# A decoder layer on one core: gathering and starting the first expert tile inside the last batch's attention heads

## The chip, the cores and the metric

The kernel runs on one core of one Trainium2 chip. The metric is the device time of one execution in microseconds, the median of several runs. It is written in Bass: every engine has its own instruction stream in program order, and streams meet only in semaphores. TensorE is PE in the rows, VectorE DVE, ScalarE ACT, GpSimd POOL, SyncE SP.

## What is computed

One post-norm decoder layer over 16 sequences of 100 tokens with 256 features, in fp32: windowed self-attention, cross-attention to 361 context rows with 16 heads, and a mixture of 8 experts of which each token takes 2.

```python
def reference(x, ctx_1024, ...):
    x = _layernorm(x + _L0_attn_ref(x, ...))
    x = _layernorm(x + _L0_xattn_ref(x, ctx_1024, ctx_1024, ...))
    x = _layernorm(x + _L0_ffn_ref(x, ...))
    return x

def _L0_ffn_ref(x, Ws, bs, Wg, Wu, Wd):
    logits = xt @ Ws + bs
    topk_w, topk_idx = jax.lax.top_k(logits, K)          # K = 2 of E = 8
    topk_w = jax.nn.softmax(topk_w, axis=-1)
    combine = jnp.sum(jax.nn.one_hot(topk_idx, E) * topk_w[..., None], axis=1)
    h = jax.nn.silu(xt @ Wg[e]) * (xt @ Wu[e])           # for every expert e, 256 -> 688
    out = sum over e of (h @ Wd[e]) * combine[:, e]
```

## The kernel before

The run has three stages.

**Self-attention** takes the 16 batches in eight pairs and leaves x1 and its transpose in DRAM.

**Cross-attention** is a software pipeline, written out by hand: iteration `i` runs 16 heads, and between the heads stand, at fixed places, the key scores and the exponentials of batch `i`, the query scores (for the maxima) and values of batch `i + 1`, the keys and queries of batch `i + 2`, and the tail of batch `i - 1`: last heads weighed (`weigh_values`), turned (`turn_weighed`), divided by the softmax sums on VectorE (`normalise`), turned again (`turn_attended`), projected (`project`), residual, mean and variance, the inverse root on GpSimd, `apply` (which makes x2), the store of x2 to DRAM, `turn_x2`, and the router product `logits`. The last iteration in which TensorE runs heads is `i = NB - 1 = 15`: there no batch is left for query scores, keys, queries or values. After it follows a stretch written out by hand for every engine, in which the tail of batch 15 is mixed with the first expert tiles.

**Routing** runs beside this in five groups of batches (`GROUPS`). Per group: logits with bias, comparison of all pairs, the two best experts (`chosen`, array `M`), ranks of the tokens within their experts (`rank_rows`, on TensorE), the place of each (`scaled`, `place`, `rounded`, `split`), one-hot rows (`hot`) and their product, the lists of tokens by tile (`enter`). Four tiles that are already full after eight batches, `Step(0, 0)` to `Step(0, 3)`, are known at the end of iteration 14 (`first_tiles` writes their rows `gat` and experts `expert_of`); they use rows of the first 800 tokens only. The other 28 tiles of `TILES = 32` are known after the last batch: `used`, `number_tiles`, `select`, `pack`.

**Expert tiles.** A tile is 128 tokens of one expert. For a tile `t`: `weights` loads 1.4 MB of gate and up weights into one of four buffers `W` (SyncE's queue); `gather` copies the tile's token numbers and issues an indirect DMA of its 128 rows of x2 from DRAM into one of four slots `xs` (GpSimd's queue); `turn_rows` transposes the rows on TensorE into PSUM bank `B_X` and `rows_out` copies them to SBUF on ScalarE; `gate_up` makes three parts of products, 4, 3 and 4 chunks of 128 columns (part 0 the gate, in bank `B_G`, part 1 the mixed one in `B_C`, part 2 the up part in `B_U`; a chunk is four passes in the trace, since fp32 takes two for each of two halves of the features); `silus` is the activation on ScalarE, `hidden` the product of both on VectorE; `down` is the product with the down weights in SBUF (`WD`), after a load of the expert's number into a register; `weigh` scales it by the token's weight and an indirect DMA adds it to DRAM. In the loop TensorE does, for `u = 0, 1, ...`: part 0 of tile `u + 2`, `down(u)`, `turn_rows(u + 3)`, and parts 1 and 2 of tile `u + 2`.

What sets the order around the change: TensorE is in order, so a `turn_rows` that waits for a gather holds everything behind it. In before, the turning of tile 0 stands right behind the router product of batch 14, after the heads. GpSimd is in order too: in iteration 15 it does `split_maximum(15, 1)`, the weights of routing group 2, the sum of x1 and bias (L1326), then the inverse root of batch 14 (L1338, L1340), constants of the tile stage (L654 to L658), and then the four early gathers (L664, L667). On SyncE the weights of tiles 0 and 1 are loaded at the start of iteration 15, x2 of batch 14 is stored, then the weights of tiles 2 and 3 follow.

## Time and profile before

| | before |
|---|---|
| median of 3 runs (lowest to highest) | 691.37 us (690.7 to 695.07) |
| the profiled execution | 694.28 us, its span 692.5 us |
| TensorE busy | 630.1 us (91%) |
| VectorE, ScalarE, GpSimd busy | 376.0, 312.4, 284.1 us |
| chain that ended last | TensorE 75%, VectorE 10%, DMA 3%, GpSimd 3% |
| mean granted TensorE clock | 0.962 |

How to read it: a busy share is an average over three stages. Self-attention goes to about 120 us of the span, cross-attention to about 408, the expert tiles to about 675, and a last normalisation follows. In a timeline a row is a group of equal instructions that follow each other, with the start, the time from first start to last end, and in brackets the idle time ahead of it and what ended it. The end of a matmul is modelled and lies somewhat behind the start of the next one, so a stretch of TensorE is best measured from start to start.

### The profile page before, as it was taken

The page shows a single profiled execution, that of the slowest core. Times are in us where ns is not written, and L with a number is a line of the kernel's source. Part 1 is how long each engine was busy: PE and PEld are TensorE (multiplying, and loading weights), DVE is VectorE, ACT ScalarE, POOL GpSimd, SP SyncE. Part 2 cuts the span into 40 slices and gives each one's busy share as a digit, 9 for nine tenths or more (in the row PEclk, how much of TensorE's full clock was granted, in tenths as well). Part 3 has the DMA queues.
Part 4 walks back from the last instruction along what each step waited for, and adds up shares of the span by engine and source line. Part 5 has one row for each costly group of instructions (what it writes and reads, how often), then busy time and mean ns, then how long its engine had stood idle before and what let it go on. Part 6 is the DMA issues. An engine that isn't in the chain of part 4 may idle for free.

```text
span 692.5 us, 16844 instructions
## 1 busy us (share of the span) xinstructions
PE 630.1 (91%) x5898; PEld 535.7 (77%) x5899; DVE 376.0 (54%) x989; ACT 312.4 (45%) x807; POOL 284.1 (41%) x511
## 2 busy tenths in 40 slices
PE   6989886999999998999899858999999999999970
PEld 5988874667777776777677648999999999999960
DVE  2878775777777876787777737222222222222214
ACT  2344424477777765777667645121221222122213
POOL 2535354333353449343954241443344334432220
PEclk9999988899999999999999979999999999999995
DMA  8332103556666644444343282877767777677105
GB/s 244 101 81 68 53 25 102 162 177 188 191 191 190 188 130 122 135 122 115 104 105 96 64 312 87 289 208 223 234 216 203 219 233 230 196 216 240 39 0 190
DMA packets 73666, 108.85 MB, mean 157 GB/s; under 512 B 9786, under 2 KB 51330, under 8 KB 72834
## 3 DMA queue, kind: packets, MB, share of 16 engines
q1 hardware_dynamic: 67458, 100.40, 46.9%
q0 software_dynamic: 6144, 7.61, 6.2%
q8 instruction: 38, 0.62, 0.4%
q14 instruction: 26, 0.21, 0.1%
HBM read 73.25 MB, written 12.44 MB: 124 GB/s over the span
## 4 chain that ended last, share of the span: by engine, by line
PE 75%; DVE 10%; issue 4%; ACT 3%; DMA 3%; POOL 3%; SPq 1%; DVEq 0%; POOLq 0%; ACTq 0%
PE ps L727 22%; PE ps L768 12%; PE ps L1459 6%; PE ps L1511 6%; PE ps L1533 5%; PE ps L1486 5%; PE ps L1470 4%; PE ps L1554 2%; PE ps L1519 2%; PE ps L1379 2%; POOL r_ln L353 1%; PE ps L1436 1%; PE ps L1390 1%; PE ps L707 1%; DVE a_mx L1988 1%
## 5 line engine op out<-in xcount | busy, mean ns | idle before, releaser
L1999 DVE TENSOR_REDUCE cmx<-ps 100x1 f32<-100x361 f32 x256 | 134.5, 531 | 68.5 <-PE ps L1459 64.2
L727 PE MATMUL ps<-xsT,W 128*128 128x128 f32 x1408 | 165.2, 276 | 0.0
L727 PEld LDWEIGHTS ps<-xsT,W 128*128 128x128 f32 x1408 | 161.3, 193 | 0.4 <-issue 0.3
L1771 ACT ACTIVATE cpr<-ps 128x300 f32<-128x300 f32 x256 | 104.8, 420 | 58.1 <-PE ps L1470 57.5
L910 DVE TENSOR_SCALAR y<-ps,wt 128x256 f32<-128x256 f32 x32 | 15.5, 484 | 143.3 <-PE ps L768 135.0
L685 POOL DMA_INDIRECT accd<-y,si x32 | 51.2, 1600 | 102.1 <-DVE y L910 101.3
L1459 PE MATMUL ps<-st 96*100 96x361 bf16 x256 | 86.0, 339 | 5.5 <-DVE cmx L1999 2.3
L768 PE MATMUL ps<-WD,hT 128*128 x384 | 88.3, 380 | 1.4 <-DVE y L910 1.4
L1470 PEld LDWEIGHTS ps<-st 120*128 120x128 bf16 x768 | 63.1, 102 | 32.1 <-issue 9.2
L1470 PE MATMUL ps<-st 120*128 120x100 bf16 x768 | 77.1, 209 | 3.6 <-ACT st L1776 1.7
L768 PEld LDWEIGHTS ps<-WD,hT 128*128 128x128 f32 x384 | 70.5, 190 | 10.0 <-issue 1.8
L1288 POOL COPY parts<-parts 128x722 bf16<-128x722 bf16 x32 | 28.5, 891 | 77.8 <-DVE parts L2006 77.8
L800 ACT ACTIVATE sg<-ps 128x512 f32<-128x512 f32 x32 | 19.1, 597 | 91.0 <-PE ps L727 91.0
L1533 PE MATMUL ps<-cwv_sb,cx 128*128 128x256 f32 x192 | 54.0, 405 | 0.0
L1459 PEld LDWEIGHTS ps<-st 96*100 96x100 bf16 x256 | 32.5, 127 | 24.8 <-DVE cmx L1999 13.3
L1511 PE MATMUL ps<-cx,cwk_sb 128*128 128x361 f32 x128 | 49.2, 509 | 0.0
L1486 PE MATMUL ps<-cpr,cva 128*32 128x100 f32 (+1 forms) x1536 | 47.6, 257 | 0.0
L667 POOL DMA_INDIRECT xs<-x2d,gi x32 | 32.8, 1025 | 25.6 <-POOL gi L664 25.6
L792 ACT ACTIVATE wt<-xs 128x8 f32<-128x8 f32 x32 | 6.7, 208 | 68.8 <-PE ps L707 68.8
L1486 PEld LDWEIGHTS ps<-cpr,cva 128*32 128x32 f32 (+1 forms) x1536 | 33.1, 111 | 5.5 <-issue 0.5
L1533 PEld LDWEIGHTS ps<-cwv_sb,cx 128*128 128x128 f32 x192 | 34.1, 197 | 2.9 <-issue 0.2
L1253 POOL TENSOR_TENSOR xb<-x_sb,bv_bc 100x512 f32<-100x512 f32 x8 | 10.2, 1275 | 48.8 <-DVE a_xr L1952 43.1
(238 smaller groups left out, 1020.0 us busy)
## 6 DMA issues: line engine op xcount, KB each, us to landing
W<-in_wgu SPq DMA_DIRECT2D x32, 1408.0 KB, 8.0
st<-parts SPq DMA_DIRECT2D x192, 115.2 KB, 2.5
WD<-in_wd SPq DMA_DIRECT2D x6, 1024.0 KB, 5.7
cx<-in_ctxT SPq DMA_DIRECT2D x16, 361.0 KB, 4.4
x_sb<-in_x SPq DMA_DIRECT2D x8, 200.0 KB
x1d<-x SPq DMA_DIRECT2D x8, 200.0 KB
x1Td<-x1T SPq DMA_DIRECT2D x8, 200.0 KB, 3.3
x1T_sb<-x1Td SPq DMA_DIRECT2D x16, 100.0 KB, 3.9
```

The costliest lines, as they stand in the source:

```text
L667: pool.indirect_dma_start(self.xs[:, t.slot, :], None, self.x2d[0:known, :], bass.IndirectOffsetOnAxis(ap=self.gi[:, t.slot:t.slot + 1], a ...
L685: pool.indirect_dma_start(self.accd, bass.IndirectOffsetOnAxis(ap=self.si[:, t.par:t.par + 1], axis=0), self.y[:, t.par, :], None, compute ...
L727: mm = pe.matmul(out[:, i * P:(i + 1) * P], self.columns(t, k, c), self.xsT[:, t.par, k, :], start=(k == 0), stop=(k == KC - 1))
L768: mm = pe.matmul(ps[:, self.B_Y, 0:D], hT[:, t.par, c, :], WD[:, c, bass.ds(e, 1), :], start=(c == 0), stop=(c == FC - 1))
L1288: pool.tensor_copy(parts[:, m, 0:3:2, 0:CTX], parts[:, m, 4:5, 0:CTX].to_broadcast([P, 2, CTX]))
L1459: pe.matmul(ps[0:L, B_S + h % 2, 0:CTX], st[b % NX][0:SR, h, CTX:KQ], st[b % NX][0:SR, h, 0:CTX], start=True, stop=True).then_inc(s_mm, 1)
L1470: mm = pe.matmul(ps[:, B_T + h % 2, c * L:(c + 1) * L], st[b % NX][:, h, FROM[c]:FROM[c] + P], st[b % NX][:, h, CTX:KQ], start=True, stop= ...
L1486: mm = pe.matmul(ps[j * VC:(j + 1) * VC, B_O, g * L:(g + 1) * L], va[b % 2][0:n, c, h, :], pr[0:n, h % (2 * HG), c * L:(c + 1) * L], start ...
L1511: mm = pe.matmul(ps[:, M0 + m, 0:CTX], wk_sb[:, k, m * P:(m + 1) * P], cx[b % NX][:, k, :], start=(k == 0), stop=(k == KC - 1))
L1533: mm = pe.matmul(ps[:, bank, o:o + D], cx[b % NX][:, k, FROM[c]:FROM[c] + P], wv_sb[:, k, :], start=(k == 0), stop=(k == KC - 1))
L1771: act.activation(pr[:, h % (2 * HG), :], ps[:, B_T + h % 2, 0:NCH * L], ACT.Exp).then_inc(exp_ok, 1)
L1999: dve.tensor_reduce(mx[:, half, hh:hh + 1], ps[0:L, B_S + h % 2, 0:CTX], AX_X, ALU.max).then_inc(max_ok, 1)
```

## The change

The three first gathers move from behind the constants on GpSimd to the place before the inverse root of batch 14, with the waits that guard them; the fourth stays behind the constants. SyncE loads the weights of tile 0 at the old place, those of tile 1 after the store of x2 of batch 14, those of tile 2 when the gather of tile 1 has landed, and those of tile 3 when the gather of tile 3 has. TensorE turns tile 0's rows at head 12 of iteration 15, into PSUM bank `M2` (the usual bank is still in use by the key scores), and makes its gate part at heads 14 and 15; ScalarE copies the rows at head 13. Behind the heads the expert work is dealt out anew between the steps of the last batch: tile 0's up part now stands ahead of the rank rows of group 3, and tile 2's gate part, which belonged to the first step of the loop, comes before the packing. VectorE takes tile 0's two hidden products earlier: the small one ahead of group 3's one-hot rows, the large one ahead of the last batch's routing.

```diff
-    def turn_rows(self, pe, t):
+    def turn_rows(self, pe, t, bank=B_X):
...
-    def rows_out(self, act, t):
+    def rows_out(self, act, t, bank=B_X):
...
         def emit(t, n):
-            if n + 1 < TILES:
+            if 1 < n < TILES - 1:
                 self.gate_up(pe, t + 1, 0, 0, 4)
...
                         sp.wait_ge(R.full_ok, 8)
                         X.weights(sp, Step(0, 0))
-                        X.weights(sp, Step(0, 1))
...
                     if i == NB - 1:
+                        X.weights(sp, Step(0, 1))
+                        sp.wait_ge(X.xs_in[1], 16)
                         X.weights(sp, Step(0, 2))
                         for u in range(2):
                             sp.wait_ge(kq_in[u], 16 * SLOTS * NB)
                         sp.wait_ge(t_mm, H * (NB - 1))
                         sp.wait_ge(v_mm, 2 * NB)
+                        sp.wait_ge(X.xs_in[3], 16)
                         X.weights(sp, Step(0, 3))
...
+                    if i == NB - 1:
+                        for u in range(2):
+                            pool.wait_ge(kq_in[u], 16 * SLOTS * NB)
+                        pool.wait_ge(t_mm, H * (NB - 1))
+                        pool.wait_ge(v_mm, 2 * NB)
+                        pool.wait_ge(R.x2_out, 32 * GROUPS[1][1])
+                        pool.wait_ge(R.full_ok, 8)
+                        for u in range(3):
+                            X.gather(pool, Step(0, u), GROUPS[1][1] * L)
...
                     if i == NB - 1:
-                        for u in range(2):
-                            pool.wait_ge(kq_in[u], 16 * SLOTS * NB)
-                        pool.wait_ge(t_mm, H * (NB - 1))
-                        pool.wait_ge(v_mm, 2 * NB)
                         X.constants(pool)
-                        pool.wait_ge(R.x2_out, 32 * GROUPS[1][1])
-                        pool.wait_ge(R.full_ok, 8)
-                        for u in range(4):
-                            X.gather(pool, Step(0, u), GROUPS[1][1] * L)
+                        X.gather(pool, Step(0, 3), GROUPS[1][1] * L)
...
+                        if h == 12 and i == NB - 1:
+                            pe.wait_ge(mT_ev[1], NB)
+                            X.turn_rows(pe, Step(0, 0), M2)
+                        if h == 14 and i == NB - 1:
+                            pe.wait_ge(max_ok, H * NB)
+                            X.gate_up(pe, Step(0, 0), 0, 0, 2)
+                        if h == 15 and i == NB - 1:
+                            X.gate_up(pe, Step(0, 0), 0, 2, 4)
...
+                        if h == 13 and i == NB - 1:
+                            X.rows_out(act, Step(0, 0), M2)
...
                 logits_out(NB - 2)
-                X.rows_out(act, Step(0, 0))
                 weighed_out(NB - 1)
+                R.grown(act, 3)
                 attended_out(NB - 1)
                 X.rows_out(act, Step(0, 1))
-                R.grown(act, 3)
...
                             if h == 14:
+                                X.hidden(dve, Step(0, 0), 1)
                                 R.denominator(dve, 3)
...
-                X.hidden(dve, Step(0, 0), 1)
+                X.hidden(dve, Step(0, 0), 2)
                 dve.wait_ge(lg_ev, NB)
                 R.biased(dve, 4)
...
                 R.which(dve, 4)
-                X.hidden(dve, Step(0, 0), 2)
```

TensorE's order, before, from head 12 of iteration 15 on: L1470 are key scores, L1486 weighed values, L1572 the router, L1561 the turning of x2, L707 the turning of a tile's rows, L727 gate and up products, L1542 the turning of the weighed values, L359 list products.

```order
L1572 MATMUL ps<-ws_sb,x2T 100x8 x2
L1470 MATMUL ps<-st 128x100 x3
L1486 MATMUL ps<-cpr,cva 32x100 x12
L1470 MATMUL ps<-st 128x100 x3
L1561 MATMUL ps<-ident,x 128x100 x2
L1470 MATMUL ps<-st 128x100 x3
L1572 MATMUL ps<-ws_sb,x2T 100x8 x2
L707 MATMUL ps<-ident,xs 128x128 x2
L1486 MATMUL ps<-cpr,cva 32x100 x12
L727 MATMUL ps<-xsT,W 128x128 x4
L1542 MATMUL ps<-ident,oT 100x128 x4
```

The same place after the change (four lines were added above, so that L1474 is the former L1470, and so on):

```order
L1576 MATMUL ps<-ws_sb,x2T 100x8 x2
L707 MATMUL ps<-ident,xs 128x128 x2
L1474 MATMUL ps<-st 128x100 x3
L1490 MATMUL ps<-cpr,cva 32x100 x12
L1474 MATMUL ps<-st 128x100 x3
L1565 MATMUL ps<-ident,x 128x100 x2
L727 MATMUL ps<-xsT,W 128x128 x4
L1474 MATMUL ps<-st 128x100 x3
L727 MATMUL ps<-xsT,W 128x128 x4
L1576 MATMUL ps<-ws_sb,x2T 100x8 x2
L1490 MATMUL ps<-cpr,cva 32x100 x12
L359 MATMUL ps<-r_ln,r_vt 104x128 x8
```

The turning of tile 0's rows has moved ahead of the last four heads' work, and its eight gate products (sixteen passes) stand between the scores of heads 14 and 15 and the router product.

TensorE, the stretch from the last projection to the turning of batch 15's x2, before (L428 to L436 are the rank rows of group 3):

```order
L1554 MATMUL ps<-cwo_sb,atT 100x256 x2
L727 MATMUL ps<-xsT,W 128x128 x4
L428 MATMUL ps<-r_Mt,r_ones 100x24
L430 MATMUL ps<-r_first,r_ones 100x24
L434 MATMUL ps<-r_M,r_ones 100x16
L434 MATMUL ps<-r_M,r_ones 100x8
L436 MATMUL ps<-r_M,r_earlier 100x24
L727 MATMUL ps<-xsT,W 128x128 x8
L1561 MATMUL ps<-ident,x 128x100 x2
```

The same stretch of TensorE after the change:

```order
L1558 MATMUL ps<-cwo_sb,atT 100x256 x2
L727 MATMUL ps<-xsT,W 128x128 x8
L428 MATMUL ps<-r_Mt,r_ones 100x24
L430 MATMUL ps<-r_first,r_ones 100x24
L434 MATMUL ps<-r_M,r_ones 100x16
L434 MATMUL ps<-r_M,r_ones 100x8
L436 MATMUL ps<-r_M,r_earlier 100x24
L1565 MATMUL ps<-ident,x 128x100 x2
```

Eight products stand ahead of the rank rows, and none between them and the turning of x2.

GpSimd in iteration 15, before (L300 routing weights, L1326 x1 and bias, L1338 and L1340 the inverse root):

```order
L1326 TENSOR_TENSOR x1b<-x1b,cbc 100x256
L1338 TENSOR_SCALAR cve<-cmv 100x1
L1340 TENSOR_TENSOR crstd<-cve,mhalf 100x1
L654 MEMSET hT 128x2x128
L655 IOTA spare 128x1
L656 MEMSET feps 128x1
L657 MEMSET fmv 128x2
L658 MEMSET warm 128x1
L664 COPY gi<-gat 128x1
L667 DMA xs<-x2d,gi 128x264
```

The same place on GpSimd after the change:

```order
L1328 TENSOR_TENSOR x1b<-x1b,cbc 100x256
L664 COPY gi<-gat 128x1
L667 DMA xs<-x2d,gi 128x264
L664 COPY gi<-gat 128x1
L667 DMA xs<-x2d,gi 128x264
L664 COPY gi<-gat 128x1
L667 DMA xs<-x2d,gi 128x264
L1349 TENSOR_SCALAR cve<-cmv 100x1
L1351 TENSOR_TENSOR crstd<-cve,mhalf 100x1
```

Three gathers stand ahead of the inverse root of batch 14.

## Rows read from the trace of the kernel before

**Rows 1.** Busy time by stretch: PE, PEld, DVE, ACT, POOL, then clock, DMA share, GB/s.

```profile
407.00:408.00 1.00, 0.59 (x10) 0.44 (x7) 0.11 (x1) 0.86 (x3) 0.48 (x1) 1.00 0.78 184
408.00:409.00 1.00, 0.42 (x4) 0.32 (x3) 0.30 (x3) 0.28 (x2) 0.98 (x2) 0.57 0.52 132
```

**Rows 2.** Timeline of PE, 397 to 418: start, us, engine, line, operation.

```profile
397.89 0.73 PE L1486 MATMUL ps<-cpr,cva 128*32 128x100 f32 x24
...
399.24 0.64 PE L1542 MATMUL ps<-ident,oT 128*100 128x128 f32 x4 [0.25 <-ACT oT L1814]
...
405.91 0.29 PE L1470 MATMUL ps<-st 120*128 120x100 bf16 x3
...
407.84 0.58 PE L1572 MATMUL ps<-ws_sb,x2T 128*100 128x8 f32 x4 [0.41 <-ACT x2T L1825]
413.59 0.66 PE L707 MATMUL ps<-ident,xs 128*128 128x128 f32 x2 [5.17 <-DMA xs<-x2d,gi]
414.18 1.23 PE L1486 MATMUL ps<-cpr,cva 128*32 128x100 f32 x24
...
417.21 1.06 PE L1542 MATMUL ps<-ident,oT 128*100 128x128 f32 x4
```

**Rows 3.** Timeline of POOL, 397 to 436.

```profile
397.93 0.75 POOL L1326 TENSOR_TENSOR x1b<-x1b,cbc 100x256 f32<-100x256 f32 x1
405.03 0.22 POOL L1338 TENSOR_SCALAR cve<-cmv 100x1 f32<-100x1 f32 x1 [6.35 <-DVE cmv L2038]
...
406.31 0.26 POOL L664 COPY gi<-gat 128x1 int32<-128x1 int32 x1
407.52 1.27 POOL L667 DMA_INDIRECT xs<-x2d,gi  x1 [0.95 <-POOL gi L664]
...
434.63 1.09 POOL L667 DMA_INDIRECT xs<-x2d,gi  x1 [0.81 <-POOL gi L664]
```

**Rows 4.** Line L667, issue to landing: the gather at 407.5; the 24 from 451.7.

```profile
DMA to landing us min/median/max: 5.9/5.9/5.9
...
DMA to landing us min/median/max: 6.2/6.9/7.8
```

**Rows 5.** Timeline of PE, 418 to 444.

```profile
418.67 1.11 PE L727 MATMUL ps<-xsT,W 128*128 128x128 f32 x8
...
420.46 1.03 PE L1554 MATMUL ps<-cwo_sb,atT 128*100 128x256 f32 x4
...
422.63 2.03 PE L727 MATMUL ps<-xsT,W 128*128 128x128 f32 x16
424.50 0.34 PE L1561 MATMUL ps<-ident,x 100*128 100x100 f32 x2
...
426.81 0.21 PE L735 MATMUL ps<-r_ones,r_Mv 100*104 100x1 bf16 x1 [1.03 <-DVE r_Mv L261]
...
430.70 0.21 PE L747 MATMUL ps<-u,r_low 104*104 104x1 bf16 x1 [0.56 <-DVE uf L862]
...
435.80 2.76 PE L768 MATMUL ps<-WD,hT 128*128 x12
...
443.52 2.76 PE L768 MATMUL ps<-WD,hT 128*128 x12
```

**Rows 6.** Timelines of DVE, 400 to 430, and of ACT, the copy of tile 0's rows.

```profile
400.21 0.42 DVE L2025 TENSOR_TENSOR at<-ps,crc 100x256 f32<-100x256 f32 x1
...
401.75 0.24 DVE L352 TENSOR_SCALAR r_vt<-r_tiles,r_vb 100x104 f16<-100x104 f16 x1
...
423.65 0.41 DVE L2044 TENSOR_SCALAR x<-at,cmv,crstd 100x256 f32<-100x256 f32 x1
...
428.74 0.17 DVE L240 TENSOR_TENSOR r_M<-r_col,r_cst 100x8 bf16<-100x8 f32 x1
...
429.20 0.69 DVE L899 TENSOR_TENSOR hT<-sg,ps 128x512 f32<-128x512 f32 x1
...
414.40 0.37 ACT L793 ACTIVATE xsT<-ps 128x256 f32<-128x256 f32 x1
```

More of the change, by code:

```diff
@@ L706, in turn_rows @@
         for k in range(KC):
-            mm = pe.transpose(self.ps[:, self.B_X, k * P:(k + 1) * P], self.xs[:, t.slot, k * P:(k + 1) * P], self.ident[:, :])
+            mm = pe.transpose(self.ps[:, bank, k * P:(k + 1) * P], self.xs[:, t.slot, k * P:(k + 1) * P], self.ident[:, :])
         mm.then_inc(self.xT_mm, 1)
@@ L792, in rows_out @@
         act.activation(self.wt[:, t.slot, :], self.xs[:, t.slot, D:XW], ACT.Copy)
-        act.activation(self.xsT[:, t.par, :, :], self.ps[:, self.B_X, 0:KC * P].rearrange("p (k t) -> p k t", k=KC),
+        act.activation(self.xsT[:, t.par, :, :], self.ps[:, bank, 0:KC * P].rearrange("p (k t) -> p k t", k=KC),
                        ACT.Copy).then_inc(self.xT_ev, 1)
@@ L1679, in _ @@
                             turn_x2(i - 1)
+                        if h == 12 and i == NB - 1:
[6 more added lines that the diff above has]
+                            X.gate_up(pe, Step(0, 0), 0, 2, 4)
                 logits(NB - 2)
-                pe.wait_ge(exp_ok, H * NB - 1)
-                X.turn_rows(pe, Step(0, 0))
                 weigh_values(NB - 1, NG - 1)
-                pe.wait_ge(max_ok, H * NB)
-                pe.wait_ge(mT_ev[1], NB)
-                X.gate_up(pe, Step(0, 0), 0, 0, 2)
+                R.enter_group(pe, 2, lists)
                 turn_weighed(NB - 1)
-                pe.wait_ge(exp_ok, H * NB)
-                R.enter_group(pe, 2, lists)
-                X.gate_up(pe, Step(0, 0), 0, 2, 4)
+                X.gate_up(pe, Step(0, 0), 1, 0, 2)
                 turn_attended(NB - 1)
                 X.turn_rows(pe, Step(0, 1))
-                X.gate_up(pe, Step(0, 0), 1, 0, 1)
+                X.gate_up(pe, Step(0, 0), 1, 2, 3)
                 project(NB - 1)
-                X.gate_up(pe, Step(0, 0), 1, 1, 3)
+                X.gate_up(pe, Step(0, 0), 2, 0, 4)
                 R.rank_rows(pe, 3, rank)
-                X.gate_up(pe, Step(0, 0), 2, 0, 4)
                 turn_x2(NB - 1)
                 X.turn_rows(pe, Step(0, 2))
+                X.gate_up(pe, Step(0, 1), 0, 0, 1)
                 logits(NB - 1)
+                X.gate_up(pe, Step(0, 1), 0, 1, 4)
+                X.gate_up(pe, Step(0, 1), 1, 0, 3)
                 X.count_first(pe)
-                X.gate_up(pe, Step(0, 1), 0, 0, 4)
                 for k in range(2 * GROUPS[3][0], 2 * GROUPS[3][1]):
@@ L1707, in _ @@
                 X.count_last(pe)
-                X.gate_up(pe, Step(0, 1), 1, 0, 1)
+                X.gate_up(pe, Step(0, 1), 2, 0, 2)
                 X.number_tiles(pe)
-                X.gate_up(pe, Step(0, 1), 1, 1, 3)
+                X.gate_up(pe, Step(0, 1), 2, 2, 4)
+                X.gate_up(pe, Step(0, 2), 0, 0, 2)
                 for k in (2 * NB - 2, 2 * NB - 1):
@@ L1713, in _ @@
                 mm.then_inc(X.route_mm, 1)
-                X.gate_up(pe, Step(0, 1), 2, 0, 2)
+                X.gate_up(pe, Step(0, 2), 0, 2, 4)
                 X.pack(pe)
-                X.gate_up(pe, Step(0, 1), 2, 2, 4)
                 X.tensor(pe)
@@ L1924, in _ @@
                 x2T_out(NB - 1)
+                X.rows_out(act, Step(0, 2))
                 logits_out(NB - 1)
@@ L1928, in _ @@
                 X.warm_up(act, ACT.Silu, 3)
-                X.rows_out(act, Step(0, 2))
                 X.silus(act, Step(0, 1), 0)
```

## The prediction

> **What bounds the kernel now.** I read the views in this order: the busy shares of the page, TensorE's timeline around the hand-over from the last batch's attention to the expert tiles, what the other engines do there, and then the waits of the gathers. TensorE is busy over nine tenths of the whole run, and in the tile loop it never waits: one tile's down product starts at 435.80 and the next at 443.52, 7.72 us apart, with no idle time marked [rows 5]. The one large hole lies between the two stages. After the router product at 407.84 TensorE stands 5.17 us until the first tile's gathered rows have landed, and only then turns them at 413.59 [rows 2]. The gather was issued at 407.52 and took 5.9 us to land [rows 3, 4]: GpSimd came to it late, since in its order the gathers stand behind the square root of batch 14, which starts when its input comes, 405.03, and behind constants. Nothing that is queued behind the wait on TensorE needed the gather (the last batch's weighing of values was ready), but its queue is in order.
>
> The hole costs a second time. The granted clock is 1.00 in 407 to 408, 0.57 in 408 to 409 [rows 1], so it goes from 2.4 to 1.2 GHz just before the hole. The work after the hole runs at the low one until the eight gate passes at 418.67, which are back at 1.11 us [rows 5]: from 413.59 to 417.21 two transposes, 24 small products and eight gate passes take 3.62 us [rows 2], where at full rate they take half of that, 1.81; the turning of the weighed values takes 1.06 us against 0.64 one batch before. That is 1.8 + 0.4 = 2.2 us lost.
>
> **The change, part by part.** I lay the new order on the times of before, from start to start, with durations at full clock.
>
> 1. First gather. GpSimd is free at 397.93 + 0.75 = 398.7 [rows 3], and everything that the gather waits for is older than that (the first tiles' list is written at the end of batch 14's iteration). Six waits stand in front; I add 0.3, an estimate. From the copy of the indices to the issue it is 407.52 - 406.31 = 1.2, so the issue starts at 400.2, and with 5.9 the rows are there at 406.1; TensorE began 0.17 after the landing, so 406.3. Bounds: the 24 gathers of the loop took 6.2 to 7.8 [rows 4]; with 7.8 it is 408.2. I take 5.9, the nearest row, since the second weight load has been moved out of its way.
>
> 2. Heads 12 to 15. TensorE comes to the turning at 405.91 [rows 2] and waits 0.4. Two transposes (half of the 0.59 from 413.59 to 414.18) are 0.3: 406.6. Scores, weighing and the turning of x2 take what they took from 405.91 to 407.43 (407.84 less its wait of 0.41), less 0.3 for the last scores: 407.8. The first gate passes wait for ScalarE's copies of about 0.2 and 0.37 [rows 6], behind the exponential of head 13: 407.9. Eight gate passes are 0.93 (half of 1.87 for sixteen [rows 5]). Twice eight, the scores of head 15 (0.15) and the router product (0.35): the weighing of the last four heads starts at 410.3, where it was 414.18.
>
> 3. The last batch's chain. From weighing to the turning of the weighed values it took 399.24 - 397.89 = 1.35, from there to the end of VectorE's scaling 400.21 + 0.42 - 399.24 = 1.4 [rows 2, 6]: 413.1. Eight gate passes and eight list products fit beside it. From 418.67 eight gate passes, then turning, two transposes and four gate passes led to the projection at 420.46 [rows 5], 0.84 without the eight: the projection is at 413.95, 6.5 earlier.
>
> 4. A wait that is new. Before, projection, eight gate passes and the rank rows take 2.17 (420.46 to 422.63), then sixteen gate passes cover VectorE, which ends the normalising at 423.65 + 0.41 = 424.06, 1.43 after the rank rows; x2 is turned at 424.50 [rows 5, 6]. Now the sixteen stand ahead of the rank rows, and VectorE cannot place or normalise before these. Rank rows done: 413.95 + 2.17 + 0.93 = 417.05; x2 turned at 418.6, after an open wait of 1.5. Still 5.9 earlier.
>
> 5. The last routing. VectorE's mask of the last batch was 428.74 - 423.65 = 5.1 after the normalising [rows 6]. Now the big product of the hidden values (about 0.6 of its 0.69 in step) stands in front: 418.1 + 5.1 + 0.6 = 423.8, done at 423.95. TensorE has turning (0.4), 28 gate passes (3.3), the router (0.35) and list products (0.45) till then: 423.1, so it waits 0.9. The 1.03 wait at 426.81 is gone. The tile numbering comes 430.70 - 428.74 - 0.6 = 1.4 after the mask, 425.2, just when eight gate passes end, so the wait of 0.56 goes too.
>
> 6. To the first down product. 24 gate passes (2.8), two list products and the packing (0.3) give 428.3. Before, 24 passes stood between packing and down product and covered the load of the expert's number; sixteen of them now come earlier in the order (tile 2's gate part). I put 0.4 for the uncovered load; between nothing and the 0.95 that GpSimd needs from a copy to its use [rows 3]. So 428.7, where it was 435.80 [rows 5]: **7.1 us earlier**.
>
> As a cross-check by the idle times: removed are 5.17, 0.41, 1.03 and 0.56 and 2.2 of slow clock, 9.4; added 0.4, 0.1, 1.5, 0.9 and 0.4, 3.3 from start to start, of which about 0.16 each is the modelled tail of the matmul before: 2.5. That is 6.9.
>
> Costed at nothing: three gathers ahead of GpSimd's square root (three times 2.0 from 399.3 end at 405.4, and it started at 405.03 [rows 3]; the 0.4 is covered, since x2 of batch 14 is turned only at 407.4). The later weight loads: tile 1's goes out at about 407.1 and is wanted at 419, tile 2's at 408.3 for 426, tile 3's behind the fourth gather at about 414 for 434. ScalarE's 0.5 us of copies lie inside TensorE's gate passes.
>
> After that the loop is TensorE's own and moves as a whole, if tile 4 is fed: its gather started at 434.63 [rows 3], 1.6 after the packing (435.80 less the 2.8 of 24 passes), so now 429.9; it lands at the latest 7.8 later, 437.7, and is turned one tile and one down product (7.72 + 2.6) after the first down product, 439.0. The cover is 1.3 us.
>
> The profiled execution took 694.28 us with a span of 692.5, 2.9 above the median of the runs, 691.37; nothing in the part that moves depends on that. So 694.3 becomes 687.2, and the median **684.3**.
>
> **Rivals.**
>
> *The clock falls all the same (0.16).* For: it fell at about 408.1, before the hole and with TensorE still 0.59 busy in 407 to 408 [rows 1], after heads of small products; those heads stay as thin, with only two transposes put in. Against: gate passes now begin at 407.9. In before, 4.7 us of work after the hole ran slow and lost 2.2; some of it would now fall into the waits. Price 1.5 to 2.2: 686.2.
> The Trainium skill ("TensorE: Matmul & The Clock Gate", Part 1) has the clock throttled after idle time and released by sustained work. By that rule the new kernel, with no hole, keeps 2.4 GHz and this rival would be out; the trace disagrees in part, with a clock that fell while the engine was mostly busy, so the rival keeps its chance.
>
> *The first gather is late (0.10).* The waiting TensorE stands at head 12 with scores, weighing, and through these ScalarE's exponentials behind it. The bound of 7.8 puts it at 408.2: 1.9 later, 686.2. For: GpSimd would now make the gather's list while VectorE runs fp16 comparisons from 401.0 to 402.6 like the one at 401.75 [rows 6]; before, the hole left VectorE idle for most of the issues. The first issue took 1.27 [rows 3], from 400.2 to 401.5; begun anew behind the comparisons it ends 1.6 later or less, 685.9.
> The Trainium skill ("SBUF — State Buffer", Who interferes with whom) says that a VectorE tensor_scalar in a two-port mode locks GpSimd out of the port by which it writes a gather's descriptors. No row of before has an early gather beside such comparisons, so it stays a rival.
>
> *The feed of tile 4 or the routing chain gives something back (0.05).* If VectorE's steps in 4 and 5 each come half a microsecond later, or tile 4 eats its 1.3 of cover: 685.5.
>
> *Better (0.12).* The two new waits rest on sums of VectorE's steps; if they come out half as long, 1.2 more is gained: 683.1.
>
> *Slower (0.03).* One mechanism: the wait now stands inside the attention heads, so a gather that lands after 406.3 + 7.1 = 413.4, 13.2 us after its issue, costs more than was gained. It would have to queue behind tile 0's whole weight load on the busy DMA engines. At 16 us: 694. No row has a gather above 7.8.
>
> *Not done as said (0.02).* One of the six waits opens only near 406, and the gathers stay where they are: 690 to 691.
>
> **How the numbers follow.** The forecast holds 0.52 with an own range of 682.8 to 686.0. This kernel's measurement can tell about 1%, here 6.9 us or 684.5, from no change. Somewhat over half of the forecast (0.30) and the better case (0.12) make faster by over 1% 0.42; the rest of the forecast (0.22), the clock, the late gather, the feed (0.31 together) and half of not done (0.01) make 0.54 within 1%; slower by over 1% is 0.04, the slower rival and the other half. The range, 682.2 to 688.2, takes in the better case, the prices of the clock and of the late gather alone and most of both together.
>
> **What would show it.** In the changed profile: the first gather's issue near 400.2, landing near 406.1; no idle time above 0.5 before the turning at head 12; the clock at 1.00 from 407 to 419; new waits of about 1.5 before x2 is turned and 0.9 at the last rank rows; packing near 428.3 and the first down product near 428.7; tiles still 7.72 apart. Wrong would be: a granted clock of 0.50 anywhere in 405 to 420, a turning after 407, a gap before tile 4 is turned.

## The result and the profile after

The changed kernel takes 689.26 us (median of 12 runs) where the kernel before, run beside it, takes 695.58 (median of 12, the first three being those of the table above). The ratio is 0.9915, with an interval of 0.9886 to 0.9945: 5.9 us faster, between 3.8 and 7.9, which is within 1% of no change. One run of 902.77, at a granted clock of 0.651, stands in that median and is left out of the ratio. A second measurement of the same kernel (r1 below) gave 0.9897, 0.9863 to 0.9931. The profiled execution took 688.24 us with a span of 686.5, against 694.28 and 692.5: 6.0 less.

The forecast of 684.3 was 5.0 too low, and its range, up to 688.2, missed the time by 1.1 us. The gain was forecast as 7.1; the two medians differ by 6.3.

TensorE's timeline of the changed kernel, to be laid beside [rows 2, 5] (start, us, engine, line, operation, idle time before and who ended it):

```profile
398.57 0.73 PE L1490 MATMUL ps<-cpr,cva 128*32 128x100 f32 x24
...
403.28 0.31 PE L1474 MATMUL ps<-st 120*128 120x100 bf16 x3 [1.31 <-ACT st L1783]
...
406.79 0.31 PE L1474 MATMUL ps<-st 120*128 120x100 bf16 x3 [0.88 <-ACT cpr L1778]
407.01 0.49 PE L1576 MATMUL ps<-ws_sb,x2T 128*100 128x8 f32 x4
407.35 0.42 PE L707 MATMUL ps<-ident,xs 128*128 128x128 f32 x2
...
408.83 1.13 PE L727 MATMUL ps<-xsT,W 128*128 128x128 f32 x8
...
411.26 0.73 PE L1490 MATMUL ps<-cpr,cva 128*32 128x100 f32 x24
...
414.95 1.03 PE L1558 MATMUL ps<-cwo_sb,atT 128*100 128x256 f32 x4
...
419.50 0.39 PE L1565 MATMUL ps<-ident,x 100*128 100x100 f32 x2 [1.34 <-DVE x L2052]
...
425.07 0.21 PE L436 MATMUL ps<-r_M,r_earlier 100*100 100x8 bf16 x1 [0.92 <-DVE r_M L240]
...
426.29 0.21 PE L747 MATMUL ps<-u,r_low 104*104 104x1 bf16 x1
...
429.29 0.18 PE L753 MATMUL ps<-sel,listed 104*128 104x28 f16 x1
...
430.03 1.34 PE L768 MATMUL ps<-WD,hT 128*128 x5 [0.46 <-issue]
```

The turning of tile 0 (L707) now stands at 407.35, and no idle time is marked before it: the hole of 5.17 is gone. In its place are idle times of 1.31 and 0.88 in the heads, 1.34 before x2 is turned, 0.92 at the last rank rows and 0.46 before the first down product.

The granted clock is 1.00 where it had been 0.57 [rows 1] (columns as there):

```profile
407.00:408.00 1.00, 1.00 (x20) 0.91 (x21) 1.00 (x5) 0.53 (x3) 0.53 (x6) 1.00 0.35 59
408.00:409.00 1.00, 1.00 (x30) 0.85 (x23) 0.09 (x1) 0.80 (x4) 0.66 (x1) 1.00 0.55 164
```

GpSimd's timeline, beside [rows 3]. The first gather is issued 7.1 us earlier:

```profile
400.44 1.27 POOL L667 DMA_INDIRECT xs<-x2d,gi  x1 [0.95 <-POOL gi L664]
...
402.78 1.01 POOL L667 DMA_INDIRECT xs<-x2d,gi  x1 [0.82 <-POOL gi L664]
...
404.78 0.97 POOL L667 DMA_INDIRECT xs<-x2d,gi  x1 [0.79 <-POOL gi L664]
405.98 0.23 POOL L1349 TENSOR_SCALAR cve<-cmv 100x1 f32<-100x1 f32 x1 [0.23 <-issue]
```

One length is used from here on: **the stretch**, from the weighing of batch 14's last heads (398.57) to the first down product (430.03). Clock episodes far from the change move whole profiles by some microseconds, and the stretch is free of them (the span of e1 below is 692.5, like that of before, though its stretch is 3.64 shorter). It is 31.46 after and 37.91 before, 6.45 less. The rest of the span's 6.0 is 0.68 lost ahead of the stretch, where nothing was changed, and 0.23 gained behind it. The loop is as it was, 7.72 us from the second down product to the third (437.85, 445.57).

### The profile page after: what moved, and what is told of

Its sections match the earlier page's. It is cut to its first block, busy times and chain, and to the rows that moved or that the text cites. A ratio compares the mean times of both kernels' runs of the same rounds, so it can differ in the third digit from the quotient of the medians.

```text
span 686.5 us, 16841 instructions
## 1 busy us (share of the span) xinstructions
PE 627.9 (91%) x5898; PEld 534.2 (78%) x5899; DVE 375.5 (55%) x989; ACT 312.1 (45%) x807; POOL 285.9 (42%) x511
## 4 chain that ended last, share of the span: by engine, by line
PE 76%; DVE 10%; issue 4%; ACT 3%; POOL 3%; DMA 2%; SPq 1%; DVEq 0%; ACTq 0%; POOLq 0%
PE ps L727 23%; PE ps L768 12%; PE ps L1463 6%; PE ps L1515 6%; PE ps L1537 6%; PE ps L1490 5%; PE ps L1474 5%; PE ps L1558 2%; PE ps L1523 2%; PE ps L1383 1%; POOL r_ln L353 1%; PE ps L1440 1%; PE ps L1394 1%; DVE a_mx L1996 1%; DVE s L1991 1%
## 5 line engine op out<-in xcount | busy, mean ns | idle before, releaser
L727 PE MATMUL ps<-xsT,W 128*128 128x128 f32 x1408 | 164.0, 275 | 0.0
L727 PEld LDWEIGHTS ps<-xsT,W 128*128 128x128 f32 x1408 | 160.5, 192 | 0.1
L1474 PEld LDWEIGHTS ps<-st 120*128 120x128 bf16 x768 | 63.2, 102 | 32.9 <-issue 9.2
L1474 PE MATMUL ps<-st 120*128 120x100 bf16 x768 | 77.1, 209 | 4.4 <-ACT cpr L1778 2.0
L681 POOL COPY si<-sca 128x1 int32 (+1 forms) x32 | 5.9, 184 | 91.2 <-DMA accd<-y,si 91.1
L667 POOL DMA_INDIRECT xs<-x2d,gi x32 | 32.9, 1029 | 25.6 <-POOL gi L664 25.6
```

The costliest lines, as they stand in the source:

```text
L667: pool.indirect_dma_start(self.xs[:, t.slot, :], None, self.x2d[0:known, :], bass.IndirectOffsetOnAxis(ap=self.gi[:, t.slot:t.slot + 1], a ...
L727: mm = pe.matmul(out[:, i * P:(i + 1) * P], self.columns(t, k, c), self.xsT[:, t.par, k, :], start=(k == 0), stop=(k == KC - 1))
L1474: mm = pe.matmul(ps[:, B_T + h % 2, c * L:(c + 1) * L], st[b % NX][:, h, FROM[c]:FROM[c] + P], st[b % NX][:, h, CTX:KQ], start=True, stop= ...
```

## Experiments

Profiled stretches, and the time against before where it was measured in rounds. A stretch stands for one profiled execution, so where it is given once nothing shows how far it repeats. Of the three kernels that were profiled twice two came again within 0.04, and the third 0.74 apart (r2 below).

| kernel | stretch us | ratio to before |
|---|---|---|
| before | 37.91 | 1 |
| the change | 31.46, again 31.42 | 0.9915 [0.9886, 0.9945], again 0.9897 [0.9863, 0.9931] |
| e1 gathers alone | 34.27 | 0.9923 [0.9892, 0.9954] |
| e2 order alone | 40.45 | 1.0045 [1.0023, 1.0067] |
| e3 rank rows first | 30.50 | |
| e4 comparisons later | 30.48 | |
| e5 gathers clear | 33.31 | |
| e6 e3 + gathers clear | 31.82 | 0.9947 [0.9927, 0.9967] |
| e7 e6 + e4 | 30.91 | 0.9901 [0.9873, 0.9930] |
| e8 gates after the heads | 34.16 | |
| e9 e3 + e4, gathers clear again | 28.87, again 28.88 | 0.9853 [0.9821, 0.9885], again 0.9887 [0.9856, 0.9918] |
| e10 e3 + e4 | 28.88, again 29.62 | 0.9884 [0.9845, 0.9924], again 0.9875 [0.9839, 0.9911] |
| e11 e9 + split gates | 28.90 | 0.9874 [0.9846, 0.9903] |

**e1, gathers alone.** Before, with GpSimd's and SyncE's part of the change:

```diff
+                    if i == NB - 1:
...
+                        for u in range(3):
+                            X.gather(pool, Step(0, u), GROUPS[1][1] * L)
```

> The kernel before with only GpSimd's and SyncE's part of the change: gathers 0 to 2 at head 2, gather 3 behind the constants, weight loads 1 to 3 later. TensorE, ScalarE and VectorE keep the order of before. Measure: the stretch from the weighing of batch 14's last heads to the first down product, 37.91 us in the profile of before, 31.46 in that of the change. Theory A (the hole of 5.17 and the slow clock of 2.2 both come from the late gather, the new order of TensorE only trades waits): the turning of tile 0 follows the router product without a wait, the clock stays 1.00, the stretch is 30.6 to 31.8, about the whole gain of the change. Rival B (the clock falls because the heads are thin; the gate passes among them are what keeps it up): the clock falls near 408 as before, the hole goes but 2.2 stays lost, stretch 32.7 to 34. Rival C (the order has to be changed for the gathers to pay): stretch over 34.

Measured: 34.27. By its mechanism this is rival B: the hole goes and the clock falls, though later than said, at 411.8 and not near 408. By its number it lies just above B's 34, partly because the waits in the heads had grown by 0.73, as they did in the change. TensorE's timeline and two stretches of busy time of e1:

```profile
411.03 0.30 PE L1474 MATMUL ps<-st 120*128 120x100 bf16 x3
411.78 0.83 PE L1576 MATMUL ps<-ws_sb,x2T 128*100 128x8 f32 x4 [0.45 <-issue]
412.46 0.67 PE L707 MATMUL ps<-ident,xs 128*128 128x128 f32 x2
...
414.22 2.08 PE L727 MATMUL ps<-xsT,W 128*128 128x128 f32 x8
```

```profile
411.00:412.00 1.00, 0.55 (x8) 0.40 (x6) 0.00 (x0) 0.96 (x3) 0.90 (x1) 0.91 0.39 129
412.00:413.00 1.00, 1.00 (x6) 0.73 (x6) 0.14 (x1) 0.22 (x2) 0.00 (x0) 0.50 0.67 103
```

The rows were there in time, yet the clock went to 0.50 (1.2 GHz) at 411.8 and eight gate passes took 2.08. Ahead of the fall lie waits of 1.30 (ahead of 405.75), 0.86 (ahead of 409.25) and 0.45, none near 5, and the change has the first two as well, 1.31 and 0.88, without a fall. So the slow clock of before was not the hole's doing alone. The waits of 1.03 and 0.56 at the last routing, which the new order removes, are still there. The early gathers give 3.64 us of the 6.45 in the stretch. The times do not tell e1 from the change: 0.9923 against 0.9915 and 0.9897, with intervals that overlap.

**e2, order alone.** The change with GpSimd's and SyncE's order of before.

```diff
-                        for u in range(3):
-                            X.gather(pool, Step(0, u), GROUPS[1][1] * L)
...
+                        for u in range(4):
+                            X.gather(pool, Step(0, u), GROUPS[1][1] * L)
```

> The changed kernel with GpSimd's and SyncE's order of before: gathers behind the square root and the constants, near 407.5, everything else as changed. Mine: the rows land near 413.5, TensorE stands at head 12 for some 7 us with scores and weighing behind it; the waits of the exponentials beside the gathers (0.76) go; the clock falls in the wait. Stretch 38.5 to 41, that is slower than before by 1 to 3 us. Rival (the order by itself fills the holes of the last routing and is worth 1 or 2): stretch 36 to 37.5.

Measured: 40.45, as said, and 0.45% slower than before, with an interval that lies above 1. TensorE waits for the rows with half a batch behind it:

```profile
414.67 0.66 PE L707 MATMUL ps<-ident,xs 128*128 128x128 f32 x2 [7.30 <-DMA xs<-x2d,gi]
```

In the stretch the halves give -3.64 and +2.54 apart, together -6.45. The change is the pair.

**e3, rank rows first, and e4, comparisons later.**

```diff
-                X.gate_up(pe, Step(0, 0), 2, 0, 4)
                 R.rank_rows(pe, 3, rank)
+                X.gate_up(pe, Step(0, 0), 2, 0, 4)
```

> The changed kernel with the rank rows of the last full group put back ahead of the last sixteen gate passes of tile 0, as in before. Mine (the wait of 1.34 before batch 15's x2 is turned comes from the rank rows standing behind those passes): VectorE normalises at about 418.2 rather than 419.04, the wait is 0.5, the stretch 31.46 - 0.85 = 30.6, with no part of it given back at the last routing, since VectorE works without a gap from the normalising to the mask. Rival (the normalising waits for GpSimd's square root or the projection): wait and stretch unchanged, 31.4. Rival (TensorE then waits more at the last rank rows): stretch 31.1 to 31.4, with the wait there grown from 0.92 to 1.4.

```diff
-                                for k in range(2 * GROUPS[3][0], 2 * GROUPS[3][1]):
+                                for k in range(2 * GROUPS[3][0], 2 * GROUPS[3][0] + 3):
                                     R.hot(dve, k)
...
-                for k in (2 * NB - 2, 2 * NB - 1):
+                for k in range(2 * GROUPS[3][0] + 3, 2 * NB):
                     R.hot(dve, k)
```

> The changed kernel with three of the last full group's six fp16 comparison pairs on VectorE (0.38 us each) moved from ahead of the last batch's mask to behind its inverse, with their list products on TensorE. Mine (the wait of 0.92 at the last rank rows is VectorE's queue: everything from the normalising to the mask runs without a gap): the mask comes 1.1 earlier, the wait goes to below 0.1, the first down product 0.9 earlier, stretch 31.46 - 0.9 = 30.55. Rival (the last batch's logits or the SiLU table loads bound the chain): the mask moves less and the stretch is 31.0 or more. Rival (the wait comes back at the numbering or at the packing): stretch 31.2 to 31.5.

Measured: 30.50 (mine said 30.6) and 30.48 (30.55). TensorE's timeline of e3: the wait before x2 is cut from 1.34 to 0.35, that at the last rank rows stays at 0.92, since VectorE's whole queue has moved by the same time:

```profile
412.02 2.03 PE L727 MATMUL ps<-xsT,W 128*128 128x128 f32 x16
414.40 0.40 PE L1565 MATMUL ps<-ident,x 100*128 100x100 f32 x2 [0.35 <-DVE x L2052]
...
419.97 0.21 PE L436 MATMUL ps<-r_M,r_earlier 100*100 100x8 bf16 x1 [0.92 <-DVE r_M L240]
```

In e4 it is the other way round, and no wait is left from x2 to the packing:

```profile
417.27 0.39 PE L1565 MATMUL ps<-ident,x 100*128 100x100 f32 x2 [1.34 <-DVE x L2052]
...
421.69 0.21 PE L436 MATMUL ps<-r_M,r_earlier 100*100 100x8 bf16 x1
...
422.91 0.20 PE L747 MATMUL ps<-u,r_low 104*104 104x1 bf16 x1
```

**e5, gathers clear of the weighings.** The change had waits in the heads that the forecast did not have: 1.31 and 0.88 where before had 1.05 and 0.38. ScalarE is late there, and not by its own doing. Two rows of before, from its timeline (the key scores of heads 10 and 11, and the exponentials from head 10 on), then the same two of the change:

```profile
404.52 0.44 PE L1470 MATMUL ps<-st 120*128 120x100 bf16 x6
...
404.87 1.24 ACT L1771 ACTIVATE cpr<-ps 128x300 f32<-128x300 f32 x3 [0.48 <-PE ps L1470]
```

```profile
405.47 0.44 PE L1474 MATMUL ps<-st 120*128 120x100 bf16 x6
...
406.32 1.24 ACT L1778 ACTIVATE cpr<-ps 128x300 f32<-128x300 f32 x3 [0.97 <-PE ps L1474]
```

From scores to exponential it is 0.35 before and 0.85 after. The trace's semaphore events put the delay at the weighing in front of the scores: it reports its end 0.95 after the start of its last product, against 0.29 elsewhere, and everything behind it on TensorE reports late too. The three weighings that do so (0.71, 0.95, 1.39) stand beside gather issues, and each report comes 0.2 to 0.5 us after the issue ends. Such a weighing is called held below.

```diff
-                        for u in range(3):
-                            X.gather(pool, Step(0, u), GROUPS[1][1] * L)
+                        pool.wait_ge(pv_mm, NG * (NB - 1) + 1)
+                        X.gather(pool, Step(0, 0), GROUPS[1][1] * L)
...
+                        pool.wait_ge(pv_mm, NG * (NB - 1) + 3)
+                        X.gather(pool, Step(0, 1), GROUPS[1][1] * L)
+                        pool.wait_ge(pv_mm, NG * NB)
+                        X.gather(pool, Step(0, 2), GROUPS[1][1] * L)
                         X.gather(pool, Step(0, 3), GROUPS[1][1] * L)
```

> The changed kernel with the gathers' issues kept clear of TensorE's weighing products: gather 0 waits for the first weighing of batch 15, gather 1 for its third, gathers 2 and 3 for its fourth. In the profile of the change three weighings report their end 0.42, 0.66 and 1.1 us later than the 0.29 that they take elsewhere, each time until 0.2 to 0.5 us after a gather's issue ends; in the profile of before none does. Theory H (a gather's issue holds up a weighing beside it): all report after 0.29, the waits at the scores of head 8 and of head 12 come back to 1.05 and 0.38, the stretch is 31.46 - 0.76 = 30.7 (within 0.2). Rival W (the traffic of the weight load or of the rows holds them): the first and the second are late as before, stretch 31.2 to 31.6. Rival S (it is ScalarE or the new order of TensorE): the same.

Measured: no late report and the waits of before, as theory H said; but the stretch grew to 33.31 (the last row is busy time by stretch):

```profile
402.01 0.31 PE L1478 MATMUL ps<-st 120*128 120x100 bf16 x3 [1.05 <-ACT st L1787]
...
405.03 0.31 PE L1478 MATMUL ps<-st 120*128 120x100 bf16 x3 [0.38 <-ACT cpr L1782]
...
413.62 0.44 PE L707 MATMUL ps<-ident,xs 128*128 128x128 f32 x2 [0.93 <-DMA xs<-x2d,gi]
...
419.75 0.39 PE L1569 MATMUL ps<-ident,x 100*128 100x100 f32 x2 [1.34 <-DVE x L2056]
...
420.95 4.55 PE L727 MATMUL ps<-xsT,W 128*128 128x128 f32 x24
...
421.00:422.00 1.00, 1.00 (x9) 1.00 (x8) 1.00 (x6) 0.85 (x2) 0.00 (x0) 0.75 1.03 411
```

Gather 1, issued at 408.0 and so 0.5 ahead of the second weight load (408.52), took 5.6 to land, where the change's gather 3, issued 1.3 ahead of that load, took 3.4. And the clock went to 0.50 at 421.5, after the wait of 1.34: 24 passes took 4.55 where the change takes 2.92. The change has the same wait with no such fall in its profile, but waits of 0.93 and 0.62 that it does not have came before it here. No run shows which of the waits the fall needs.

**e6 and e7, first attempts to beat both.** e6 is e3's edit with gather 0 held as in e5, gather 1 behind the square root, gathers 2 and 3 behind the last weighing; e7 adds e4's edit.

```diff
+                        X.gather(pool, Step(0, 1), GROUPS[1][1] * L)
                         X.constants(pool)
+                        pool.wait_ge(pv_mm, NG * NB)
+                        X.gather(pool, Step(0, 2), GROUPS[1][1] * L)
                         X.gather(pool, Step(0, 3), GROUPS[1][1] * L)
```

> A version meant to beat both: the changed kernel with the rank rows ahead of the sixteen passes (as in e3), gather 0 held until the first weighing of batch 15 is done (as in e5), gather 1 right behind the square root, gathers 2 and 3 behind the last weighing. Mine: no weighing is held up, gather 1 lands before the second weight load gets going (by 411, where e5 had it at 413.6 on its scale), the clock stays 1.00, stretch 31.46 - 0.95 (e3 measured) - 0.7 = 29.8; time 0.986 to 0.991 of before. Rival (gather 1 is late again, or it holds the third weighing): 30.3 to 31.5. Rival (the clock falls somewhere as in e5): over 31.

> As the version before, with three comparison pairs and their list products moved behind the last mask as well. Mine: a further 0.9, stretch 28.9, time 0.985 to 0.990 of before. Rival (the wait at the last rank rows had already gone or comes back at the numbering): as the version before, 29.5 to 29.9.

Measured: 31.82 and 30.91, each 2.0 worse than mine, for a reason that none of the theories had, and times of 0.9947 and 0.9901, each above the forecast. The first two weighings were not held, but the third was, beside gather 1 (1.46 and 1.50), against what was said and without a wait behind it on TensorE. The timeline of e6, GpSimd, ScalarE and TensorE together:

```profile
415.41 0.97 POOL L667 DMA_INDIRECT xs<-x2d,gi  x1 [0.79 <-POOL gi L664]
416.41 0.23 POOL L283 TENSOR_TENSOR r_ex<-r_lg,r_best 100x24 f32<-100x24 f32 x1
...
416.67 0.22 ACT L289 ACTIVATE r_ex<-r_ex 100x24 f32<-100x24 f32 x1 [3.86 <-POOL r_ex L283]
416.80 0.32 ACT L1829 ACTIVATE atT<-ps 128x200 f32<-128x200 f32 x1
...
417.17 1.11 PE L1561 MATMUL ps<-cwo_sb,atT 128*100 128x256 f32 x4 [1.79 <-ACT atT L1829]
```

The held gathers had been moved ahead of a small subtraction on GpSimd. ScalarE's exponential waits for that one, the copy of the attended values stands behind the exponential, and TensorE's projection behind the copy.

**e8, gate passes after the heads.** The change with its sixteen gate passes of heads 14 and 15 behind the heads: eight behind the last weighing and eight behind the turning of the weighed values.

```diff
-                        if h == 14 and i == NB - 1:
-                            pe.wait_ge(max_ok, H * NB)
-                            X.gate_up(pe, Step(0, 0), 0, 0, 2)
-                        if h == 15 and i == NB - 1:
-                            X.gate_up(pe, Step(0, 0), 0, 2, 4)
...
+                pe.wait_ge(max_ok, H * NB)
+                X.gate_up(pe, Step(0, 0), 0, 0, 2)
...
+                X.gate_up(pe, Step(0, 0), 0, 2, 4)
```

> The changed kernel with the sixteen gate passes of heads 14 and 15 put behind the last weighing; the early gathers and the turning at head 12 stay. In e1, whose heads hold no gate passes either, the clock fell although no wait of over 0.5 was left. Mine (gate passes among the heads are what keeps the clock up): it falls near 409 to 412, the stretch is 32.5 to 34. Rival (it was e1's late turning, the order behind the heads, and not the heads): the clock stays 1.00 and the stretch is 31.2 to 31.8.

Measured: 34.16 (mine said up to 34.0). Busy times of e8 by stretch:

```profile
409.00:410.00 1.00, 0.19 (x2) 0.20 (x3) 0.00 (x0) 0.90 (x3) 0.00 (x0) 1.00 0.76 126
410.00:411.00 1.00, 1.00 (x29) 0.83 (x28) 0.40 (x3) 0.24 (x2) 0.00 (x0) 0.93 0.82 165
411.00:412.00 1.00, 1.00 (x5) 1.00 (x6) 0.59 (x2) 0.61 (x2) 0.94 (x2) 0.50 0.96 377
```

Without the passes TensorE waits 1.33 for the copy of x2, which the held weighing delays, and is busy for 0.19 in 409 to 410; the clock falls at 410.9. The passes do two things: they fill that wait, and the clock stays up. e8 alone does not tell whether the clock needs the filled wait or the passes' own work; in e1, where it fell too, the last wait ahead of the fall was only 0.45. In none of the twelve profiles with an early first gather and the passes among the heads (the change, e3 to e7, e9 to e11, r1 to r3) did the clock fall before the projection.

**e9 to e11, better versions.** e9 has e3's and e4's edits, like e7, and places the gathers anew: gather 0 held for the first weighing, 1 and 2 behind the square root, 3 behind the residual's bias. e10 has e3's and e4's edits and the gathers of the change. e11 puts four gate passes behind e9's packing:

```diff
-                X.gate_up(pe, Step(0, 2), 0, 2, 4)
+                X.gate_up(pe, Step(0, 2), 0, 2, 3)
                 X.pack(pe)
+                X.gate_up(pe, Step(0, 2), 0, 3, 4)
```

> As e7, with the gathers placed anew. In e6 and e7 gathers 2 and 3, held for the last weighing, stood in GpSimd's queue ahead of the logits' differences that ScalarE exponentiates before it copies the last attended values, so TensorE waited 1.79 at the projection. Now gather 0 is held for batch 15's first weighing, gathers 1 and 2 follow the square root, gather 3 follows the residual's bias. Mine: the waits at the scores of head 8 and 12 are 1.05 and 0.38, none at the projection, 0.4 before x2, none at the last rank rows; the third weighing is held up by gather 1 as in the changed kernel, at no cost; the clock stays 1.00. Stretch 31.46 - 0.95 (e3) - 0.97 (e4) - 0.7 = 28.85. Rival (gather 2 holds the last weighing and the chain of the last batch with it): 29.3 to 29.9. Rival (gather 1 or 2 lands late in the weights' traffic): over 30. Time 0.984 to 0.990 of before.

> The changed kernel with e3's and e4's edits together and its gathers left where they are. Mine (the two waits are two terms that add, 0.95 and 0.97 as measured apart): stretch 31.46 - 1.92 = 29.55; time 0.985 to 0.990 of before. Rival (one wait was the other's cover, so that the second edit alone gave the same): 30.3 to 30.5.

> As e9_clear_again, with the last four gate passes of tile 2 put between the packing and the first down product. Mine (the 0.46 ahead of the first down product is the load of the expert's number, which nothing covers, as step 6 of the prediction priced at 0.4): the wait goes, and the packing, now four passes earlier, waits at most 0.1: stretch 28.45. Rival (the packing then waits for VectorE's lists, 0.4 or more): 28.8 to 28.9.

Measured: e9 28.87, as said; e10 28.88, 0.67 better than said; e11 28.90, no gain, which is the rival's number but not its reason, since the packing does not wait. The times of e9 and e10 are in the range said. e11 lost the idle time before the down product, but the down product starts 0.86 after the start of its four passes, which take about 0.44 (419.96 to 420.40 in the change's own timeline):

```profile
429.98 0.19 PE L753 MATMUL ps<-sel,listed 104*128 104x28 f16 x1
...
430.20 0.71 PE L727 MATMUL ps<-xsT,W 128*128 128x128 f32 x4
431.06 1.13 PE L768 MATMUL ps<-WD,hT 128*128 x4
```

So about 0.4 of the load of the expert's number stays uncovered behind four passes; in e1, where 24 passes stand there as in before, they start at 432.55 and the down product at 435.33, which is no more than the 2.8 that the passes need.

e10 contradicted theory H: its gather 0 stands at the same distance from the first weighing as in the change, and yet this weighing reports 0.29 after the start of its last product; the second, whose last product starts 0.26 behind the start of gather 2's issue, reports after 0.36. TensorE's rows of e10:

```profile
402.45 0.73 PE L1490 MATMUL ps<-cpr,cva 128*32 128x100 f32 x24
...
404.79 0.31 PE L1474 MATMUL ps<-st 120*128 120x100 bf16 x3 [1.05 <-ACT st L1783]
```

**r1 to r3, again on one chip** (the one that e9 to e11 ran on): the change, e10 and e9.

> The changed kernel once more, beside the two below on one chip. In the profiles so far the weighings beside a gather's issue report late in the change, e1, e3, e4 and e8 (two chips), and not in e10, whose gathers stand at the same distance from them, on a third chip. Theory K (it is the program: what e10 changed behind head 15 matters): here the change shows the waits of 1.31 and 0.88 and e10 again 1.05 and 0.38. Theory C (it is the chip or the execution): both kernels show the same, held or not; held, the stretch is 31.45 here, not held 30.8. Time 0.989 to 0.994 of before.

> The kernel of e10 once more. Theory K: stretch 28.9, waits 1.05 and 0.38 again. Theory C: held if the change is held here, then 29.55 as first forecast for e10, else 28.9. Time 1.9 us (0.3%) below the changed kernel's on this chip, either way.

> The kernel of e9 once more, to set it beside the change and e10 on one chip. Stretch 28.9 under either theory, since its gathers are clear of the first two weighings; if weighings are held here, it is 0.65 ahead of e10's kernel, if not, level with it. Time 2.5 us (0.4%) below the changed kernel's if held, 1.9 if not.

Measured: 31.42, 29.62, 28.88, which is theory C with the weighings held; e10's kernel now takes what was first forecast for it, so the two terms of e3 and e4 do add. The median times of r2 and r3 lie 3.1 and 1.9 us below r1's (said 1.9 and 2.5). The same kernel on the same chip that had shown 1.05 now shows 1.30:

```profile
396.66 0.73 PE L1490 MATMUL ps<-cpr,cva 128*32 128x100 f32 x24
...
399.25 0.31 PE L1474 MATMUL ps<-st 120*128 120x100 bf16 x3 [1.30 <-ACT st L1783]
```

So it is neither the program nor the chip but the execution: beside an early gather the first two weighings were held in all seven profiles of the change, e1, e3, e4, e8, r1 and r2, and not in that of e10. Where no gather's issue stands beside them they were never held (before, e2, e5, e6, e7, e9, e11, r3). The third weighing gives the same: with an issue beside it, it was held in nine profiles (1.37 to 1.50) and not in those of e9 (0.42) and e11 (0.35), while r3, the kernel of e9, shows 1.46. The overlap is needed, and does not always suffice. The traffic was the same: around the first weighing the DMA share was 0.75 and 1.03 in e10 (402 to 404) and 0.73 and 1.02 in r2 (396.2 to 398.2). The price of holding the first two is 0.74 of the stretch, 29.62 against 28.88 for e10's kernel.

## Why the prediction was wrong

Two steps of the sum failed: the last one, on the base, and step 2. The other terms of the gain came near what was said.

**The base.** The last step of the sum, "so 694.3 becomes 687.2, and the median 684.3", took 2.9 us off because the median of three runs was 691.37. With twelve runs it is 695.58, and in four further sets of 11 to 17 runs 693.45 to 695.51. The profiled execution was typical, the three runs were not. The same gain of 7.1 taken from 695.58 gives 688.5, 0.8 from the measured 689.26. Of the miss of 5.0 this step is 4.2, the distance between the medians of three and of twelve runs (691.37 and 695.58). It says nothing of the mechanism.

**The gain.** 6.45 us at the first down product against 7.1. By steps, on the scale of before (the change's times less 0.68):

- Step 1, first gather: issued at 399.8 (said 400.2). Its landing was mis-sized, said 5.9 after the issue: the packets of the first two gathers all lie before 406 on the change's own scale, so within 5.6 of it, and in e10 the same gather took 4.7. The turning stands at 406.67 (said 406.3), and the wait of 0.4 for rows did not occur.
- Step 2 is the term of the gain that failed: "TensorE comes to the turning at 405.91". It came 0.76 later, since the held weighings delayed the scores of heads 8 and 12. The sum had no term for what an early gather's issue does to the weighings beside it. By luck 0.4 of this had been allowed for as a wait for rows, so the last weighing is at 410.6 (said 410.3). The gain without the holding would be 6.45 + 0.74 = 7.2, by the price that e10's kernel shows.
- Step 3, projection 414.3 (413.95). Step 4, the new wait, 1.34 (1.5), x2 turned at 418.8 (418.6). e3 shows that its cause was read rightly, rank rows behind sixteen passes, and that it was worth 0.95.
- Step 5, mask 424.2 (423.8), wait 0.92 (0.9), numbering 425.6 (425.2). e4 shows the cause: VectorE's queue.
- Step 6, packing's start 428.6 (about 428.1, since 428.3 had the list products and the packing in it), idle time 0.46 (0.4), first down product 429.35 (428.7). So 0.3 of the missing 0.65 is there at the last weighing, and the rest comes in behind the turning of x2, spread over steps 5 and 6.
- The clock: the hole and the slow clock went as said, 5.17 and 2.2 us. The main text of the prediction tied the slow clock to the hole; its first rival had the other half, that the thin heads alone could bring the clock down and that the gate passes from 407.9 on stood against it. e1 shows a hole closed and a slow clock all the same, and e8 that the clock falls when those passes leave the heads. The Trainium skill ("TensorE: Matmul & The Clock Gate", Part 1) has the clock throttled after idle time and released by sustained work. e1 agrees with it only in part: its clock fell with TensorE 0.55 busy in the last microsecond, and the longest idle time in the six microseconds before was 0.86.
- The rivals: the clock did not fall. The first gather was not late; its issue took 1.27 as before, but VectorE's comparisons ran only from 401.67 on, and the two overlap by 0.04. Gather 1, from 402.78 half beside them, took 1.01, where the 32 gathers take 0.97 to 1.27, so nothing of a locked port was seen; a first issue with the comparisons ahead of it was not run. Tile 4 was fed in time. The mechanism of the slower rival, a wait for rows with the heads behind it, is real (e2), but the change's gather was not late.

## What to carry to other kernels

When a wait stands in the middle of in-order queues, changing the producer's place or the consumer's alone can bring half or less than nothing; here, in the profiled stretch, -3.6 and +2.5 apart, -6.45 together. Work moved between queues must be followed through every engine that waits behind it (e6: gather, subtraction, exponential, copy, projection). And a gain summed on one profile is to be set against that profile's own time, until there are more than three runs: their median was off by more than half of the gain.

The best version is e9's: both measurements beat before (0.9853 and 0.9887), and its stretch is 2.6 us shorter than the change's. The times hardly tell it from the change: on one chip they are 0.9887 and 0.9897, with intervals that overlap, as do those of e10 and e11. The first pair (0.9853 and 0.9915) has intervals that just miss each other, but was not measured side by side.

## What the runs showed of the hardware

- TensorE's weighing products (32-column weights, float32) report their end up to 1.2 us late (1.50 after the last product's start in e7, 1.39 in the change, against 0.29 elsewhere) when a gather is being issued on GpSimd, in most executions but not in all. Gate and down products in the loop, which run beside gathers as well, did not: in the change all of them report after 0.29 and 0.39. The Trainium skill ("SBUF — State Buffer", Who interferes with whom) states of the ports of SBUF that "PE and ACT never wait on anyone". No run here shows whether a port is behind the late reports, and what TensorE waits for stays open.
- The clock fell without a long wait: in e1 to 0.50 with TensorE 0.55 busy in the microsecond before, in e5 after an idle time of 1.34 that left it at 1.00 in the change. Neither was foreseen from waits alone.
- A gather issued 1.3 us ahead of a weight load landed 3.4 us after its issue (the change), one issued 0.5 us ahead of it 5.6 (e5).
